# An attention and feed-forward block: TensorE's order in a unit turned, Q and K packed from SBUF to SBUF, both masks kept on chip

## The reference

```python
x = x + layernorm(attention(layernorm(x), W_qkv, W_out, b_out))
x = x + layernorm(ffn(layernorm(x), W_up, W_gate, W_down))

# attention: 16 heads of 32; interleaved (q, k, v) columns in W_qkv
q = q * cos + rotate_half(q) * sin        # rotary, pairs (2d, 2d+1); the same for k
mask = (j <= i) & (j >= i - 128)          # a band of 129 keys
attn = softmax(where(mask, q @ k.T / sqrt(32), -big))
y = (attn @ v) @ W_out + b_out
# ffn: ternary weights, hidden = silu(x @ up.T) * (x @ gate.T), then @ down.T; 2048 hidden
```

## Time and profile before

| | |
|---|---|
| median of 3 runs | 1574.02 us (1569.62 to 1575.28) |
| the profiled execution | 1572.07 us, span 1570.3 us |
| granted TensorE clock, mean | 0.94 |
| busy, share of the span | TensorE 85%, VectorE 69%, ScalarE 46%, GpSimd 32% |
| attention layer | from the start to about 806 us |
| ternary weights | to about 870 us |
| feed-forward layer | to the end |

### The profile page before, as it was taken

The page is one execution under the profiler, slowest core; times in us unless marked ns, Lnnn a source line. Parts: engine busy times, 40 slices in busy tenths (PEclk is TensorE's granted clock), DMA queues, the critical chain, the costliest instruction groups (busy, mean ns, idle before and its releaser), DMA issues. The chain is left out here.

```text
span 1570.3 us, 23805 instructions
## 1 busy us (share of the span) xinstructions
PE 1337.6 (85%) x7942; PEld 732.5 (47%) x7942; DVE 1078.8 (69%) x2567; ACT 725.6 (46%) x1410; POOL 497.0 (32%) x594
## 2 busy tenths in 40 slices
PE   3678979988897897888540799999999999999995
PEld 2355646555564655555320344444444444444442
DVE  3678979888897888889729545646465555556553
ACT  1465766667666666756535223232322323232321
POOL 2535664655656456565320000102010101101011
PEclk9888989999998999999675899999999999999998
DMA  9588889889898879889834000000000000000000
GB/s 349 143 176 173 169 194 178 160 184 187 167 171 189 178 155 189 171 169 179 160 139 184 0 1 0 28 1 28 0 28 1 0 28 0 28 1 28 1 28 27
DMA packets 363769, 164.62 MB, mean 105 GB/s; under 512 B 293632, under 2 KB 348160, under 8 KB 362624
## 3 DMA queue, kind: packets, MB, share of 16 engines
q1 hardware_dynamic: 363648, 163.11, 46.1%
HBM read 64.42 MB, written 25.17 MB: 57 GB/s over the span
## 5 line engine op out<-in xcount | busy, mean ns | idle before, releaser
L587 ACT ACTIVATE prob<-prob,peak 128x256 f32<-128x256 f32 x512 | 230.6, 498 | 180.1 <-DVE peak L709 178.9
L883 PE MATMUL J<-xnT,weights 128*128 128x512 f32 x512 | 257.9, 630 | 7.9 <-ACT xnT L571 7.9
L709 DVE CUSTOM_DVE_ANT_0 prob<-S,band,neg_score_scale 128x256 f32<-128x256 f32 x512 | 226.4, 479 | 35.1 <-DMA band<-in_bands 23.8
L1127 DVE SCALAR_TENSOR_TENSOR su<-U,sig 128x512 f32<-128x512 f32 x128 | 88.5, 692 | 198.6 <-ACT sig L1063 196.8
L718 DVE SCALAR_TENSOR_TENSOR parts<-prob,parts 128x512 f16<-128x512 f32 x256 | 209.8, 820 | 19.3 <-ACT parts L595 19.1
L1063 ACT ACTIVATE sig<-U,sig_scale 128x512 f32<-128x512 f32 x128 | 88.1, 688 | 231.3 <-PE U L1205 231.3
L1205 PE MATMUL U<-xT_hi,up_q 128*128 128x512 f16 x512 | 194.6, 380 | 0.0
L1205 PE MATMUL U<-xT_lo,up_q 128*128 128x512 f16 x512 | 194.6, 380 | 0.0
L1216 PE MATMUL Y<-down_q,h_hi 128*128 128x512 fp8e4 x512 | 194.1, 379 | 0.5 <-DVE h_lo L1138 0.5
L1205 PE MATMUL G<-xT_hi,gate_q 128*128 128x512 f16 x512 | 194.0, 379 | 0.0
L1205 PE MATMUL G<-xT_lo,gate_q 128*128 128x512 f16 x512 | 194.0, 379 | 0.0
(11 more groups left out here) (122 smaller groups left out, 1980.6 us busy)
## 6 DMA issues: line engine op xcount, KB each, us to landing
spill<-split SPq DMA_DIRECT2D x64, 256.0 KB, 2.6
Qp<-spill SPq DMA_DIRECT2D x128, 128.0 KB, 2.8
Kp<-spill SPq DMA_DIRECT2D x128, 128.0 KB, 2.9
out_x<-o_sb SPq DMA_DIRECT2D x8, 1024.0 KB, 4.3
X<-in_x SPq DMA_DIRECT2D x1, 6144.0 KB, 25.7
weights<-parts SPq DMA_TRANSPOSE x256, 3.2
Kc<-Kp SPq DMA_DIRECT2D x32, 128.0 KB, 3.0
w_gate_here<-in_w_gate SPq DMA_DIRECT2D x2, 2048.0 KB, 9.7
```

What stands on the lines that cost most here:

```text
L587: e = nc.scalar.activation(prob[:, u % 4, h, :], prob[:, u % 4, h, :], ACT.Exp, bias=peak[:, u % 4, h:h + 1], scale=-1.0)
L709: e = nc.vector.tensor_tensor_reduce(out=prob[:, u % 4, h, :], in0=S_ps[u % 2][:, h * 2 * P:(h + 1) * 2 * P], in1=(band0 if first_tile els ...
L883: e = pe.matmul(dst[:], W[:, s, c, g * P:(g + 1) * P], xnT[:, c, :], start=(c == 0), stop=(c == DC - 1))
L1127: nc.vector.scalar_tensor_tensor(su[:, c % 2, :], U_ps[c % 2][:], H_SCALE / XN_SCALE ** 2, sig[:, c % 2, :], ALU.mult, ALU.mult).then_inc( ...
```

## The change

- TensorE's step does the projection pieces first, then the scores, then the values. Before, the scores came first.
- The columns of W_q and W_k are laid out on the host so that partition p of a group holds dimension p // 4 of head p % 4. `split` then has the order in which `Qp` and `Kp` take it, and four DMAs pack straight from `split`. `spill` and its DMAs are gone. The neighbour of a dimension is now 4 partitions away, so the shuffle's pattern and the layout of the tables differ.
- ScalarE may write a new high half once the pack before it has landed, where it waited for the spill's landing before.
- A pack now stands where the spill stood in `moves`, except `pack_q` of group 2, which stays at step 5. `pack_k` of group 3 moves from step 19 to 18 and so ahead of turn 19.
- `band0` and `band` are loaded once. Which one a first tile uses is fixed when the program is built.

```diff
@@ sync queue @@
             def pack_q(i, g):
                 n = i * NG + g
-                written, scored = worked_out(sp, 16 * (n + 1), (n - 1) * STEPS)
-                sp.wait_ge(q_spilled, written)
+                q_split, scored = worked_out(sp, 2 * n + 1, (n - 1) * STEPS)
+                sp.wait_ge(r_lo_done, q_split)
                 at_least(sp, score_done, scored)
                 for row, part in enumerate((0, 0, 1, 1)):
-                    sp.dma_start(Qp[row * HD:(row + 1) * HD, g % 2],
-                                 spill[0, part].rearrange("(h d) t -> d h t", h=4)).then_inc(q_packed, 16)
-            def spill_k(i, g):
...
+                    sp.dma_start(Qp[row * HD:(row + 1) * HD, g % 2], split[:, 0, part]).then_inc(q_packed, 16)
...
-            moves = {0: [(spill_k, 1, 0)], 1: [(pack_k, 1, 0)],
-                     2: [(carry_k, 0, 0)], 4: [(spill_q, 2, 0)], 5: [(pack_q, 2, 0), (carry_v, 0, 0)],
-                     6: [(spill_k, 2, 0)], 8: [(pack_k, 2, 0)],
+            moves = {0: [(pack_k, 1, 0)],
+                     2: [(carry_k, 0, 0)], 5: [(pack_q, 2, 0), (carry_v, 0, 0)], 6: [(pack_k, 2, 0)],
                      10: [(carry_k, 1, 0)], 13: [(carry_v, 1, 0)],
-                     16: [(spill_q, 3, 0)], 17: [(pack_q, 3, 0)], 18: [(spill_k, 3, 0)], 19: [(pack_k, 3, 0)],
+                     16: [(pack_q, 3, 0)], 18: [(pack_k, 3, 0)],
                      20: [(carry_k, 2, 0)], 21: [(carry_v, 2, 0)],
-                     24: [(spill_q, 0, 1)], 25: [(spill_k, 0, 1), (pack_q, 0, 1)], 26: [(pack_k, 0, 1)],
+                     24: [(pack_q, 0, 1)], 25: [(pack_k, 0, 1)],
                      27: [(carry_k, 3, 0)], 29: [(carry_v, 3, 0)],
-                     30: [(spill_q, 1, 1)], 31: [(pack_q, 1, 1)]}
+                     30: [(pack_q, 1, 1)]}
...
-                    if plan is not LAST and u == 28:
-                        used, next_tile = worked_out(sp, i * UNITS + (NG - 1) * STEPS + 2, i + 1)
-                        sp.wait_ge(logit_done, used)
-                        sp.dma_start(band0[:], row(bands, next_tile)).then_inc(band0_in, 16)
@@ scalar: rotated_high @@
-                at_least(act, (q_spilled, k_spilled)[a], 16 * n)
+                at_least(act, (q_packed, k_packed)[a], 64 * n)
@@ vector: empty @@
-                                             [d ^ 1 for d in range(HD)]).then_inc(swap_done, 1)
+                                             [p ^ 4 for p in range(HD)]).then_inc(swap_done, 1)
@@ vector: logits @@
-                if first_tile and u % 2 == 0:
-                    dve.wait_ge(band0_in, bands_in)
+                mask = band0 if first_tile and (i + u // UNITS) % PER_BATCH == 0 else band
@@ tensor: macro_tile @@
                 for u in range(UNITS):
+                    for piece in plan.steps[u]:
+                        fill(piece, i, plan)
                     if u + 2 < UNITS or plan is not LAST:
                         score(i, u + 2)
-                    for piece in plan.steps[u]:
-                        fill(piece, i, plan)
                     if u >= LAG:
                         weighted_values(i, u - LAG)
```

More of the change, by code:

```diff
@@ L255, in attention @@
         w_scale, neg_score_scale, o_scale = (sb(n, [P, 1]) for n in ("w_scale", "neg_score_scale", "o_scale"))
-        spill = nc.dram_tensor("spill", [2, 2, P, MT], F16).ap()
         S_ps = [ps("S0"), ps("S1")]
@@ L267, in attention @@
         const_in, bias_in, table_in, band0_in = sem("const_in"), sem("bias_in"), sem("table_in"), sem("band0_in")
-        q_spilled, k_spilled, q_packed, k_packed = sem("q_spilled"), sem("k_spilled"), sem("q_packed"), sem("k_packed")
+        q_packed, k_packed = sem("q_packed"), sem("k_packed")
         set_up, wmax_parts_done, wmax_done, wmax_spread, scales = (
@@ L332, in turn @@
                                        in_=parts[:, u % TURNED].rearrange("p s k -> p (s k)")).then_inc(p_turned[u % TURNED], 16)
[L334 to L339, removed]
             def pack_q(i, g):
                 n = i * NG + g
-                written, scored = worked_out(sp, 16 * (n + 1), (n - 1) * STEPS)
-                sp.wait_ge(q_spilled, written)
+                q_split, scored = worked_out(sp, 2 * n + 1, (n - 1) * STEPS)
+                sp.wait_ge(r_lo_done, q_split)
                 at_least(sp, score_done, scored)
                 for row, part in enumerate((0, 0, 1, 1)):
-                    sp.dma_start(Qp[row * HD:(row + 1) * HD, g % 2],
-                                 spill[0, part].rearrange("(h d) t -> d h t", h=4)).then_inc(q_packed, 16)
-            def spill_k(i, g):
[L351 to L355, removed]
+                    sp.dma_start(Qp[row * HD:(row + 1) * HD, g % 2], split[:, 0, part]).then_inc(q_packed, 16)
             def pack_k(i, g):
                 n = i * NG + g
-                written, scored, carried = worked_out(sp, 16 * (n + 1), (n - 1) * STEPS, 16 * (2 * i + g // 2))
-                sp.wait_ge(k_spilled, written)
+                k_split, scored, carried = worked_out(sp, 2 * n + 2, (n - 1) * STEPS, 16 * (2 * i + g // 2))
+                sp.wait_ge(r_lo_done, k_split)
                 at_least(sp, score_done, scored)
@@ L363, in pack_k @@
                 for row, part in enumerate((0, 1, 0, 1)):
-                    sp.dma_start(Kp[row * HD:(row + 1) * HD, g % 2],
-                                 spill[1, part].rearrange("(h d) t -> d h t", h=4)).then_inc(k_packed, 16)
+                    sp.dma_start(Kp[row * HD:(row + 1) * HD, g % 2], split[:, 1, part]).then_inc(k_packed, 16)
             def carry_k(i, g):
@@ L412, in row @@
                 return t[bass.ds(n, 1)].rearrange("a p k -> (a p) k")
-            spill_q(0, 0)
             pack_q(0, 0)
-            spill_k(0, 0)
             pack_k(0, 0)
-            spill_q(0, 1)
             pack_q(0, 1)
-            spill_k(0, 1)
             pack_k(0, 1)
@@ L700, in logits @@
                 first_tile = u // 2 % TT == 0
-                scored, halved, bands_in = worked_out(
-                    dve, i * UNITS + u + 1, i * UNITS + u - 3, 16 * (i + 1 + u // UNITS))
+                scored, halved = worked_out(dve, i * UNITS + u + 1, i * UNITS + u - 3)
                 settled(dve, x0_in)
@@ L710, in logits @@
                         out=prob[:, u % 4, h, :], in0=S_ps[u % 2][:, h * 2 * P:(h + 1) * 2 * P],
-                        in1=(band0 if first_tile else band)[:], scale=neg_score_scale[:], scalar=3.0e38,
+                        in1=mask[:], scale=neg_score_scale[:], scalar=3.0e38,
                         op0=ALU.add, op1=ALU.min, accum_out=peak[:, u % 4, h:h + 1])
@@ L798, in _ @@
             dve.wait_ge(bias_in, 16)
+            dve.wait_ge(band0_in, 16)
             dve.wait_ge(set_up, 5)
@@ L1357, in by_tile @@
     def by_tile(t):
-        t = np.tile(t.T.astype(np.float32), (P // HD, 1))
+        t = np.repeat(t.T.astype(np.float32), P // HD, axis=0)
         t = t.reshape(P, PER_BATCH, MT).transpose(1, 0, 2)
@@ L1369, in band_masks @@
     seen = (k >= q) & (k <= q + WINDOW)
-    masks = np.zeros((NM, P, 2 * P), np.float32)
-    for i in range(NM):
-        masks[i][~(seen & ((k >= P) | (i % PER_BATCH != 0)))] = NEG
+    masks = np.zeros((2, P, 2 * P), np.float32)
+    for i in range(2):
+        masks[i][~(seen & ((k >= P) | (i != 0)))] = NEG
     return masks
@@ L1380 @@
     cos_t, sin_t = rope_tables()
+    w_qkv = np.asarray(L0_attn_W_qkv).reshape(D, NG, 4, HD, 3)
+    w_qk = [w_qkv[..., part].transpose(0, 1, 3, 2).reshape(D, D) for part in range(2)]
     arrays = {
         "x": np.ascontiguousarray(L0_attn_x),
-        "w_qkv": np.ascontiguousarray(np.asarray(L0_attn_W_qkv).reshape(D, D, 3).transpose(2, 0, 1)),
+        "w_qkv": np.ascontiguousarray(np.stack([*w_qk, w_qkv[..., 2].reshape(D, D)])),
         "w_out": np.ascontiguousarray(L0_attn_W_out),
```

## The result

The changed kernel takes 1614.55 us (median of 4 runs, 1609.68 to 1615.73) against 1574.65 for the kernel before on the same chip, a ratio of 1.025, 95% interval 1.023 to 1.028. The prediction said 1559 in a range of 1545 to 1573. It is wrong in size and sign. Its profiled execution has a span of 1613.7 us.

The account below looks back on a forecast made before the run. VectorE's gaps were taken to bound the attention layer. Terms -4.8 (prologue), -11 (boundary), 0, -3.6 (last tile) and +4 (later score) sum to -15.4: 1572.07 becomes 1556.7, plus 1.95 to the median, said as 1559, range 1545 to 1573.

Parts of the forecast that it names:

- What bounds the kernel: Steady attention layer: VectorE is busy 46.2 of 47 us, so its gaps, not TensorE's waits, can be won.
- Bandwidth sets little: Steady attention layer: DMA engines are 91% busy, but turns land in 3.2 us against at least 3.0.
- The prologue: Before the first score: packs no longer follow two DRAM round trips, score at 49.4 instead of 54.2, gain 4.8 us.
- The boundary: Between macro tiles, seven times: mask waits go, the later first score takes part back; gain 1.6 us each, 11 in all.
- takes back about half: Second score of a macro tile: V 0's three other pieces stand ahead, costing some 1 us of the boundary's 1.7.
- Steps 20 and 21: Transposes and Q 0, seven times: unit 22's later score and the earlier cosine table cancel, 0; bounds -15.2 and +14 us.
- The last macro tile: Group 3: VectorE's 3.63 us wait for packed K 3 goes as the pack leaves earlier, gain 3.6 us.
- Everywhere else: the later score: Other steps: scores after pieces lose slack when packs precede turns; 0.06 us for each of 64, 4 us lost in all.
- The chain I had worked out: Other steps: logits through low half, turn, values, pieces and score take 13.4 to 15.5 us; six VectorE units are 15.0.
- the slack of 0.5 us against 0.7: Other steps: with pieces ahead, a score is done 0.5 us before VectorE takes it; the hand-over takes 0.7.
- Rival 3: Other steps: the later score binds, each of 64 packs makes VectorE wait 0.6 us; +19, so 1593, chance 0.08.
- Rival 4: Low halves: GpSimd and VectorE meet elsewhere; a mean moved by 0.1 us makes 26 us, 1583; chance 0.04.

Follow-up runs that it names:

- turned_30: packs_spread with the scores first, except in step 30, where TensorE's pieces go ahead of the score: 1551.86 us, 0.986 of the kernel before.
- packs_spread: The changed kernel with each direct pack's four copies divided into two pairs behind two successive turns: 1574.98 us, 1.000 of the kernel before.
- turned_but_30_31: packs_spread with the scores first in steps 30 and 31 and the pieces first in all others: 1584.43 us, 1.007 of the kernel before.
- spread_old_order: packs_spread with TensorE's old order, scores first in every step: 1563.61 us, 0.992 of the kernel before.
- extra_sbuf: The kernel before with one more copy, from SBUF to a spare SBUF tile, behind each of 256 turns: 1669.89 us, 1.061 of the kernel before.
- extra_dram: The kernel before with one more copy, from DRAM to a spare SBUF tile, behind each of 256 turns: 1679.86 us, 1.067 of the kernel before.

## Why the prediction was wrong, step by step

**What bounds the kernel** was right: VectorE's gaps. "Bandwidth sets little" held as well: turned_30 keeps the engines at 49.8% of 1550 us, 772 us each, the kernel before at 46.1% of 1570, 724, and it is faster. What I did not ask is what the queue of SyncE has left. 32 turns of 1.26 us and 32 copies of 0.60 are 59 us of a macro tile's 98 in the changed kernel. With the carries, the tables and the long turns, its DMAs hold it for 70.7 of 98.5 us in macro tiles 1 to 6, 72%; in the kernel before it was 67.1 of 91.9, 73%, and in turned_30, the fastest, 68.1 of 89.7, 76%. The Trainium skill, "Perfetto Trace Analysis", section "What 'DMA-bound' means", lists the issuing engine's sequencer as a bound of its own, apart from the 16 engines, and knows it by a track that is solid with DMA slices. The trace agrees that it is apart, but here it bound without a solid track, and its share tells the slow kernel from the fast one in no way. What tells the changed kernel from packs_spread is the longest hold between two turns, which have a due time.

**The prologue** (-4.8): -4.2 in the two traces, but 1.6 like for like; the rest is the earlier start. The step "four DMAs in 1.73 us as before" is wrong (2.54), K's block stands behind Q's, and the landing is 4.0. The estimate of 2.3 us from the Trainium skill, "SBUF — State Buffer", section "The DMA setup-cost knee", is further off still from the 3.6 and 4.3 measured.

**The boundary** (-11): right in mechanism, somewhat too large. The term was for both steps turned, and alone those give 5.9, with step 30 by itself 11.7. Inside the full order both steps give 1584.4 - 1575.0 = 9.4, and the gaps of the changed kernel are 8.9 smaller in six tiles, 10.4 for seven. The loss at the second score ("takes back about half") is right as well.

**Steps 20 and 21** (0): gaps at units 22 and 23 grow by 3.3 us in the changed kernel: unit 22 loses 12.6, unit 23 gives back 9.1. Giving this block its old order back changed nothing (+1.4). As a sum 0 was fair.

**The last macro tile** (-3.6): 1.9 at its group 3, where 1.70 of 3.63 remains, and a new gap of 3.69 at unit 12 takes it back. K's pack lands 4 us after it is sent, not 2.9.

**Everywhere else: the later score** (+4, "0.06 us for each", bounds 0 and 0.6): this is the step that failed, in two ways. The pack in one block cost 39.6 us under the new order, 0.66 for each of 60, beyond the upper bound (27.3 and 0.45 under the old). I had priced the pack's queue time at the old 1.73 and had not counted that spill and pack had been two holds of 0.54 and 1.73 with turns between, and now were one of 2.49. And the pieces first in the 30 other steps cost 20.8 with the packs in pairs, where I counted nothing without a pack. Together that is 60.4 us where the sum had 4. The chain I had worked out, 13.4 to 15.5 us in the 15.0 of six units, did say how little there was (and it had TensorE's pieces at the upper clock level alone): the row to believe was the slack of 0.5 us against 0.7, not the median of the turns.

**The masks**: no separate term, and none was there (-1, within the uncertainty).

**The rivals.** Rival 3 was the right mechanism: a block of the queue in front of a turn meets a score without slack, at 0.6 for a pack. It gave 1593 and 8 in 100. Its own sum with 60 packs at 0.66 gives -19.4 + 39.6 = +20, 1594. The 20.8 of the other steps are what it lacks to the 1614.6 measured. Rival 4 was there in part: the mean of the low half moves by 26 ns, 6.8 us. The page's groups for the two orders with packs in pairs, packs_spread first and spread_old_order second:

```profile
L693 DVE SCALAR_TENSOR_TENSOR parts<-prob,parts 128x512 f16<-128x512 f32 x256 | 216.2, 844 | 10.9 <-ACT parts L572 10.7
```

```profile
L693 DVE SCALAR_TENSOR_TENSOR parts<-prob,parts 128x512 f16<-128x512 f32 x256 | 208.9, 816 | 32.0 <-ACT parts L572 31.7
```

The gaps of these two are alike (64.0 and 66.1 in the table), and yet the new order is 11.4 slower by the medians and 7.5 in these two traces: 7.3 of it are the low halves themselves. The low halves of packs_spread wait less for ScalarE and take longer. The order of the 30 other steps does not do it by itself: turned_but_30_31 has it too, and its low halves take 209.1 us, 817 ns each. That those of packs_spread overlap more with GpSimd is what the Trainium skill, "SBUF — State Buffer", section "Who interferes with whom", would make of it. The rows show only the longer times. Which instructions of GpSimd they meet was not tried.

**What stays open.** Why the order of the other steps costs 20.8 us. Where it does is known: the gaps of turned_but_30_31 are 17 us larger than those of spread_old_order in six tiles, some 20 for seven, 9 of the 17 at units 22 and 23 and 5 at unit 15. But turning the first block back alone gained nothing, and the clock, at its lower level for 63.9 us against 54.0, may have a part. And why a direct pack's issue takes 0.60 us and its landing 3.3 to 4.4: into 128 partitions the source makes no such difference (below), into 32 it does, and no run varies the number of partitions alone. Sending packs from another engine's queue was not tried. By the Trainium skill, "Trainium Kernel Development and Optimization", section "Key Constraints", that saves issue time and nothing else. No run here shows it, but the time that the queue is held is just what these runs found short.

## What to carry to other kernels

When a queue sends something with a due time at every step, price a change by the longest hold of the queue between two such sends, and look whether four short DMAs can stand as two and two. Shares of busy time and bytes say nothing on it: this change more than halved the bytes read from DRAM (64.42 to 29.95 MB by the two pages) and lost 40 us, and the division of the same copies won them back. Before an order is turned for the sake of one place, turn it in that place alone: here step 30 by itself gave 11.7 us, while the other steps took 20.8.

## What the hardware showed that I had not expected

- A copy of 128 rows of 1 KB from SBUF into 32 partitions takes 596 ns of SyncE's queue, the same from DRAM 432. Into 128 partitions the median is alike from both sources, by the lines of extra_sbuf and extra_dram:

```profile
L395 SPq DMA_DIRECT2D spare<-Wo x256: 464/535/1742, 62.1 to 879.7; - x128
DMA to landing us min/median/max: 1.9/2.2/4.8
```

```profile
L395 SPq DMA_DIRECT2D spare<-in_w_out x256: 332/523/1938, 62.3 to 892.2; - x128
DMA to landing us min/median/max: 2.0/2.5/4.2
```

- 256 such copies behind turns cost 95 and 105 us, 0.37 and 0.41 each, most of their issue time of 0.53. Whether the queue or the engines set that, whose share rose from 46.1% to 50.0% and 51.2%, was not separated.
- Twenty waits that are met at once held the queue for 0.62 us, 31 ns each.
